# Two transfers instead of eight for each rotated projection, layer norms spread over two periods, and the MLP's gelu kept in its PSUM bank

## What is computed

```python
attn_in = adaln(x, cond, ln1, g1, b1)
x = attn(attn_in, attn_in, sa_wq, sa_wkv, sa_wo, sa_bo) + x
cross_in = adaln(x, cond, ln1, g1, b1)
x = attn(cross_in, ln(context), ca_wq, ca_wkv, ca_wo, ca_bo) + x
ffn_in = adaln(x, cond, ln2, g2, b2)
x = gelu(ffn_in @ ff_w1 + ff_b1) @ ff_w2 + ff_b2 + x

def attn(xq, ctx, ...):            # rope on q and k, softmax over 512 keys
    q, k, v = heads(xq @ wq), heads(ctx @ wk), heads(ctx @ wv)
    return softmax(rope(q) @ rope(k).T * DH ** -0.5) @ v @ wo + bo

def adaln(x, c, lw, lb, gw, gb, bw, bb):
    return ln(x, lw, lb) * (1 + c @ gw + gb) + (c @ bw + bb)
```

## Time and profile before

| | |
|---|---|
| median of 3 runs (range) | 1145.44 us (1144.98 to 1146.52) |
| the profiled execution | 1144.7 us, span of its instructions 1142.9 us |
| PE busy | 1099.4 us (96%) |
| DVE, POOL, ACT busy | 855.3, 774.0, 638.0 us (75, 68, 56%) |
| mean granted TensorE clock | 0.988 |

### The profile page before, as it was taken

How to read it: one execution, slowest core, us unless ns; L and a number is a source line. 1 busy time by engine, 2 the same in 40 slices (tenths; PEclk the granted TensorE clock), 3 DMA queues, 4 the chain that set the end, 5 groups by cost and what they waited for, 6 DMA issues and landing times.

```text
span 1142.9 us, 18646 instructions
## 1 busy us (share of the span) xinstructions
PE 1099.4 (96%) x6888; PEld 786.5 (69%) x6888; DVE 855.3 (75%) x1025; ACT 638.0 (56%) x895; POOL 774.0 (68%) x497
## 2 busy tenths in 40 slices
PE   7689999999999999999999999999999999989998
PEld 6456667776667777666766667776666667756887
DVE  5677787878787777778787777777787778676543
ACT  5455556665666555566565555555555555674521
POOL 3477788788678777688789766776777767654110
PEclk9799999999999999999999999999999999989999
DMA  6212111221221111211121112211121111300001
GB/s 183 61 30 75 38 41 45 70 48 34 51 73 40 38 38 31 59 38 38 26 64 38 38 38 50 58 33 32 31 70 38 38 38 38 93 1 1 20 19 37
DMA packets 65689, 52.36 MB, mean 46 GB/s; under 512 B 29120, under 2 KB 48576, under 8 KB 65344
## 3 DMA queue, kind: packets, MB, share of 16 engines
q1 hardware_dynamic: 63712, 49.59, 17.5%
q10 hardware_dynamic: 1888, 1.59, 0.5%
HBM read 15.22 MB, written 2.10 MB: 15 GB/s over the span
## 4 chain that ended last, share of the span: by engine, by line
PE 81%; DVE 7%; issue 4%; ACT 3%; POOL 2%; DMA 2%; SPq 2%; ACTq 0%; POOLq 0%; DVEq 0%
PE ps L862 16%; PE ps L711 11%; PE ps L712 10%; PE ps L713 10%; PE ps L809 6%; PE ps L840 5%; PE ps L850 5%; PE ps L815 5%; PE ps L811 5%; PE ps L813 4%; PE ps L945 3%; DVE neg_max L1036 2%; SPq L342 2%; DMA lo<-eo 1%; PE ps L727 1%
## 5 line engine op out<-in xcount | busy, mean ns | idle before, releaser
L537 ACT ACTIVATE probs<-ps 128x1024 f32<-128x1024 f32 x256 | 262.4, 1026 | 209.3 <-PE ps L815 185.5
L1036 DVE TENSOR_REDUCE neg_max<-ps 128x2 f32<-128x1024 f32 x256 | 301.7, 1225 | 80.9 <-PE ps L840 80.8
L412 POOL TENSOR_TENSOR acc<-acc,probs 128x1024 f32<-128x1024 f32 x128 | 304.6, 2380 | 17.7 <-POOL acc L407 0.4
L862 PE MATMUL ps<-probs,v 128*64 128x512 f32 x1024 | 230.7, 592 | 0.0
L407 POOL TENSOR_TENSOR acc<-probs 128x1024 f32<-128x1024 f32 x64 | 152.5, 2383 | 82.1 <-ACT probs L537 82.1
L417 POOL TENSOR_TENSOR eo<-tmp 128x512 f32<-128x512 f32 x62 | 89.2, 1439 | 137.9 <-DVE tmp L1063 129.0
L862 PEld LDWEIGHTS ps<-probs,v 128*64 128x64 f32 x1024 | 73.6, 137 | 145.8 <-issue 145.8
L1063 DVE TENSOR_TENSOR tmp<-ps,rope 128x1024 f32<-128x1024 f32 x128 | 150.6, 1212 | 3.5 <-PE ps L713 2.6
L809 PE MATMUL ps<-max_rows,pick 64*128 64x512 f32 x512 | 110.5, 422 | 11.1 <-DVE o_lo L1050 6.0
L840 PE MATMUL ps<-hi 64*128 64x512 f32 x512 | 106.8, 408 | 14.1 <-ACT hi L551 7.8
L711 PE MATMUL ps<-xn_hi,w_hi 128*128 128x512 f32 x256 | 108.2, 423 | 0.0
(11 more groups left out here) (113 smaller groups left out, 2269.1 us busy)
## 6 DMA issues: line engine op xcount, KB each, us to landing
lo<-eo SPq DMA_DIRECT2D x512, 64.0 KB, 2.0
w_raw<-pack_dram SPq DMA_DIRECT2D x16, 192.0 KB, 3.2
x<-x_dram SPq DMA_DIRECT2D x4, 512.0 KB, 10.8
w_raw<-pack_dram SPq DMA_DIRECT2D x8, 256.0 KB, 3.7
max_rows<-neg_max SPq DMA_DIRECT2D x128, 2.0 KB, 2.0
w_raw<-w_dram SPq DMA_DIRECT2D x2, 1024.0 KB, 5.6
out<-x SPq DMA_DIRECT2D x4, 512.0 KB, 2.9
ctx_in<-ctx_dram SPq DMA_DIRECT2D x4, 384.0 KB, 3.6
```

The costliest lines, as they stand in the source:

```text
L412: pool.tensor_tensor(acc[:, g % 2, :, :], acc[:, g % 2, :, :], probs[:, i, :, :], ALU.add).then_inc(added, 1)
L537: act.activation(probs[:, i, :, :], score_ps(i), ACT.Exp, scale=SCALE).then_inc(exped, 1)
L862: mm = pe.matmul(av_ps[DH * h:DH * h + DH, :], v[:, u % 2, kt, c:c + DH], probs[:, kt, h, :], start=(kt == 0), stop=(kt == TT - 1))
L1036: dve.tensor_reduce(neg_max[:, g % 2, :, i], peak_ps(i), AX.X, ALU.max, negate=True).then_inc(maxed, 1)
```

## The change

1. `land` issues two DMAs a job instead of eight: one for each pair, 64 partitions of `eo` with both halves, into all 128 partitions of `raw_qk`. It waits for both halves first. Rows of q and k come to lie in another order of partitions (the same in both).
2. Norms in periods: `guess_rstd` goes to behind `keep_av`, `norm_rows` to the next period, behind `guess_inverse` and ahead of `high_qk`. This holds for the context's norms too. `norm_stats` goes behind `normalise`, and `refine_rstd` behind the third `add_probs`.
3. The MLP's gelu is written back to its PSUM bank, `hid` is gone; `split_hid` reads PSUM; `hidden` waits for `hid_split`. The last two norms come one block earlier, with a gelu between their halves, and `refine_rstd(LAST)` moves from DVE to POOL.
4. The opening: 10 and 6 products of constants (`warm`) on PE; `modulate` in four parts, the second norm's two later; job 1 turned into a buffer of its own; another order on every engine; x of batch entry 3 and the context loaded later; `cols` waits apart from `ctx_ln`.

```diff
+        def eo_of(j):
+            return acc[:, 1, :, :] if j == 1 else eo
...
         def job_ps(j, e):
-            return ps[:, (2 if j == 3 else 3) + e, :]
+            return ps[:, 3 + e, :]
+        def hid_ps(f):
+            return ps[:, (f + 3) % 4, :]
         def ln_ps(n, r):
-            if n == 2:
-                return ps[:, r, :]
...
-        norm_at = {NB - 1: (0, 0, 1, True)}
+        norm_at = {NB - 1: (0, 1, 1)}
...
-            norm_at[norm_of(X, 1, b)] = (p, p, p + 1, True)
-        norm_at[norm_of(X, 2, 0)] = (PAIRS - 5, PAIRS - 5, PAIRS - 4, True)
-        norm_at[norm_of(X, 2, 1)] = (PAIRS - 3, PAIRS - 3, PAIRS - 2, True)
+            norm_at[norm_of(X, 1, b)] = (p, p + 1, p + 1)
+        norm_at[norm_of(X, 2, 0)] = (PAIRS - 5, PAIRS - 4, PAIRS - 4)
+        norm_at[norm_of(X, 2, 1)] = (PAIRS - 3, PAIRS - 2, PAIRS - 2)
...
             def land(j):
-                sp.wait_ge(rotated, 2 * j + 1)
+                sp.wait_ge(rotated, 2 * j + 2)
...
-                    for e in range(2):
-                        if a == 0 and e == 1:
-                            sp.wait_ge(rotated, 2 * j + 2)
-                        for h in range(2):
-                            rows = DH * h + 32 * e
-                            at = 32 * (2 * a + h)
-                            sp.dma_start(raw_qk[rows:rows + 32, g % 4, k, :], eo[at:at + 32, e, :])\
-                              .then_inc(landed, 16)
+                    sp.dma_start(raw_qk[:, g % 4, k, :], eo_of(j)[64 * a:64 * a + 64, :, :]).then_inc(landed, 16)
...
             load_weights(0)
-            for b in range(1, NB):
-                sp.dma_start(x[:, b, :, :], x_d[b].rearrange("(t p) d -> p t d", p=128)).then_inc(x_in[b], 16)
-            load_ctx(0)
+            load_x(1)
+            load_x(2)
             land(0)
             land(1)
             land(2)
             land_max(0)
+            load_x(3)
+            load_ctx(0)
             land(3)
...
@@ POOL, period(p) @@
                     add_probs(p, 2)
-                if n is not None and norm_at[n][3]:
-                    refine_rstd(pool, n)
                     add_probs(p, 3)
+                if p in stats_in:
+                    refine_rstd(pool, stats_in[p])
...
@@ ACT, period(p) @@
                     guess_inverse(p - 1)
+                if p in rows_in_period:
+                    norm_rows(rows_in_period[p])
                 if is_pair(p + 2):
                     high_qk(p + 2)
                 if p in split_in:
                     split_weights(*split_in[p])
-                if at_once:
-                    guess_rstd(n)
-                    norm_rows(n)
                 if is_pair(p - 1):
                     high_o(p - 1)
                 if is_pair(p):
                     keep_av(p)
+                if p in stats_in:
+                    guess_rstd(stats_in[p])
+                if p in turned_in:
+                    norm(turned_in[p], 0)
+                    norm(turned_in[p], 1)
...
             def gelu(b, f):
                 act.wait_ge(hid_mm, 8 * b + f + 1)
-                if f >= 4:
-                    act.wait_ge(hid_split, 8 * b + f - 3)
-                act.activation(hid[:, f % 4, :], ps[:, (f + 3) % 4, :], ACT.Gelu,
+                act.activation(hid_ps(f), hid_ps(f), ACT.Gelu,
...
@@ PE, opening @@
+            warm(10)
             modulate(0)
+            modulate(1)
             norm(0, 0)
             norm(0, 1)
             turn_rope()
-            modulate(1)
+            warm(6)
             project(0)
+            project(1)
             norm(1, 0)
             norm(1, 1)
-            project(1)
             project_v(0, 0)
             project_v(0, 1)
+            modulate(2)
             project(2)
+            peak(0, 0)
+            peak(0, 1)
+            peak(0, 2)
+            peak(0, 3)
+            modulate(3)
+            project(3)
             norm(2, 0)
             norm(2, 1)
-            for i in range(TT):
-                peak(0, i)
-            project(3)
...
@@ DVE, opening @@
-            modulate(1)
             rotate(0, 0)
-            norm_stats(2)
             rotate(0, 1)
             turn(0)
             rotate(1, 0)
             rotate(1, 1)
             turn(1)
+            norm_stats(2)
             rotate(2, 0)
             rotate(2, 1)
             for i in range(TT):
                 peak(0, i)
             low_qk(0)
+            modulate(1)
             rotate(3, 0)
...
@@ DVE, period(p) @@
-                if n is not None:
-                    norm_stats(n)
                 if is_pair(p - 1):
                     normalise(p - 1)
+                if p in stats_in:
+                    norm_stats(stats_in[p])
+                if is_pair(p - 1):
                     low_o(p - 1)
...
@@ PE, mlp(b) @@
                 def hidden(f):
                     if f >= 4:
-                        pe.wait_ge(hid_ready, 8 * b + f - 3)
+                        pe.wait_ge(hid_split, 8 * b + f - 3)
+                    elif b > 0:
+                        pe.wait_ge(hid_split, 8 * (b - 1) + f + 5)
```

More of the change, by code:

```diff
@@ L434, in period @@
                     add_probs(p, 2)
-                n = stats_in.get(p)
-                if n is not None and norm_at[n][3]:
-                    refine_rstd(pool, n)
-                if is_pair(p):
                     add_probs(p, 3)
-                if n is not None and not norm_at[n][3]:
-                    refine_rstd(pool, n)
+                if p in stats_in:
+                    refine_rstd(pool, stats_in[p])
                 if p in split_in:
@@ L457, in _ @@
             refine_rstd(pool, 2)
+            rotate(2)
             low_weights(pool, 0, 3)
-            rotate(2)
             norm_split(pool, 2, 0)
@@ L593, in period @@
                     split_weights(*split_in[p])
-                n = stats_in.get(p)
-                at_once = n is not None and norm_at[n][3]
-                if at_once:
-                    guess_rstd(n)
-                    norm_rows(n)
                 if is_pair(p - 1):
@@ L602, in period @@
                     keep_av(p)
-                if n is not None and not at_once:
-                    guess_rstd(n)
-                turned = turned_in.get(p)
-                turned_late = turned is not None and norm_at[turned][0] == p
-                if turned is not None and not turned_late:
-                    norm(turned, 0)
-                    norm(turned, 1)
+                if p in stats_in:
[3 more added lines that the diff above has]
+                    norm(turned_in[p], 1)
                 if p in v_in:
                     keep_v(v_in[p], 0)
-                if turned_late:
-                    norm(turned, 0)
-                if p in v_in:
                     keep_v(v_in[p], 1)
-                if turned_late:
-                    norm(turned, 1)
-                n = rows_in_period.get(p)
-                if n is not None and not norm_at[n][3]:
-                    norm_rows(n)
                 if p in (PAIRS - 3, PAIRS - 2):
@@ L670, in _ @@
             norm_rows(LAST - 1)
-            for f in range(3, 7):
-                gelu(0, f)
+            gelu(0, 3)
+            gelu(0, 4)
+            gelu(0, 5)
             norm(LAST - 1, 0)
+            gelu(0, 6)
             norm(LAST - 1, 1)
@@ L679, in _ @@
             norm_rows(LAST)
-            for f in range(1, 7):
+            for f in range(1, 6):
                 gelu(1, f)
             norm(LAST, 0)
+            gelu(1, 6)
             norm(LAST, 1)
@@ L879, in period @@
                     pe.wait_ge(maxed, 4 * (p + 1) + 4)
-                n = turned_in.get(p)
-                at_once = n is not None and norm_at[n][0] == p
-                if n is not None and not at_once:
-                    norm(n, 0)
-                    norm(n, 1)
+                if p in turned_in:
+                    norm(turned_in[p], 0)
+                    norm(turned_in[p], 1)
                 if is_job(p + 4):
@@ L896, in period, with warm @@
                     project_out(u - 1, 1)
+            def warm(count):
+                pe.wait_ge(const_ready, 6)
+                for _ in range(count):
+                    pe.matmul(ps[:, 1, :], pick[:, :], max_rows[:, :], start=True, stop=True)
+            warm(10)
             modulate(0)
+            modulate(1)
             norm(0, 0)
@@ L931, in hidden @@
                     for kt in range(KT):
-                        mm = parts(ps[:, (f + 3) % 4, :], w1_hi[:, kt, cut], w1_lo[:, kt, cut],
+                        mm = parts(hid_ps(f), w1_hi[:, kt, cut], w1_lo[:, kt, cut],
                                    xn_hi[:, b, kt, :], xn_lo[:, b, kt, :], kt == 0, kt == KT - 1)
@@ L1108, in period @@
                     rotate(p + 4, 1)
-                if n is not None and is_pair(p + 2):
+                if is_pair(p + 2) and p in stats_in:
                     low_qk(p + 2)
```

100 lines of the change are left out of this document (51 added, 49 removed).

## The result

The changed kernel takes 1118.61 us (median of 4 runs, 1118.14 to 1118.73) against 1145.45 us for the kernel before beside it: the ratio is 0.9764, 95% interval 0.9747 to 0.9781, so 27 us less. The forecast was 1119.7. The sum was right; its terms were not, and this is what the experiments are about.

What follows compares the result with a forecast made beforehand. PE's own work was taken to bound two thirds of the kernel, the prize lying in its idle time elsewhere. 13.0 + 5.0 + 2.5 + 4.5 = 25.0 off 1144.7 gave 1119.7 us, range 1111 to 1130 (own 1113 to 1124).

Steps and rivals of the forecast that it cites:

- Part 1: Two transfers a job instead of eight: 4.9 us in the opening against 6.9, 5.5 against 6.9 in the periods.
- The rival of a landing over 6.2 us: 256 KB transfers land late, PE waits in each of 32 quads and the kernel gets slower, 1177 at 8 us; chance 0.03.
- In the periods it hides behind PE: In the periods the shorter transfers save PE nothing; they only move SP's queue to the better.
- Part 2, the opening: Opening up to period 1: gains 4.6, 3.5, 4.8 and 1.3, less 1.2, sum 13.0 us.
- near 55: Sign in the opening: `score(1, 0)` would come near 55 us instead of 68.
- All 24: Jobs 0 and 1, 24 products at 0.43 us instead of 0.23: all would give 4.8 us; 3.5 taken with DVE's relief.
- Against this: `modulate(1)` and `rotate(3)` ... -1.2: Opening: both now stand between the maxima and `peak(1, 0)`, costing 1.2 us, an estimate at one rotation.
- The opening gives only half: Rival: clock stays half through jobs 0 to 1, another chain ends the opening; 13.0 becomes 6.5, 1126 us; chance 0.15.
- Part 3: Norms over two periods: 4.6 of 5.6 us idle back in 467 to 600, plus 0.4 in 68 to 467: 5.0.
- The rival of 11 new waits: Rows ahead of `high_qk` cost 0.6 us in each of 11 norms, period 62 stays as it is: 1129; chance 0.10.
- Part 4: Periods 59 to 62: PE's 4.71 us wait for `o_lo` gives 1.8, what follows 0.7: 2.5 us.
- Part 5: MLP with gelu in PSUM: 4.5 of the 5.2 us waits for `hid_lo` gained, some 0.5 left at the first `down`.

Runs made afterwards that it cites:

- period 61 turned round: Changed kernel with DVE's `low_o` ahead of `norm_stats` in period 61: 1120.67 us, ratio 0.9783, against 1118.68 for the version with `rotate(3)` ahead of `norm_split`.

## Why the forecast was right in sum and wrong in its terms

In short: the forecast of 1119.7 is near 1118.6 by luck, since its terms are off by up to 4.2 us and cancel. **The reading of the bound held.** PE was full in two thirds of the kernel, and 1 to 27 and 35 to 59 didn't move (+0.2 and -0.6). All the gain lies in the four stretches named.

**Part 1.** From the end of the turn's first half to the landing, 4.9 us was taken: 0.7 + 1.2 + 3.0. Measured: an issue 0.6, a landing 3.2 in the median and 3.6 for the second of a job, 3.8 for that of job 1, inside the bounds of 2.0 and 3.7 but for that; for job 1 the way is 6.1, since POOL held the second half of the turn. The rival of a landing over 6.2 us is out. What failed is "In the periods it hides behind PE": the two transfers alone gave 3.9 us in 27 to 35. PE's old waits there were put down to `issue` or to DVE, and I read them as the norms' alone; ACT's 10.0 us of waiting for landings stood behind them.

**Part 2, the opening: 13.0 forecast, 8.8 measured.** Marks of before against after: `hi` 40.82 and 33.86; first scores 51.15 and 46.71; pair 0's average 56.66 and 53.10; `score(1, 0)` 68.08 and 60.49 (the sign "near 55" was missed); pair 1's average 75.32 and 66.55. So, step by step:

- up to `hi`: 7.0 of the forecast 4.6 + 3.5 = 8.1. The turn of job 1 starts at 26.97, where the working gives 30.6 - 3.5 = 27.1, but it takes 2.5 instead of 1.4, and its landing 3.8 instead of 3.0. The split in two terms was wrong: the own buffer is worth 0.5 to 0.8 by its run, not the 3.07 of the old wait, since with two transfers the landing that it waited for comes sooner, and DVE is held by POOL where it would have waited. "All 24" products at half clock was wrong too: in the kernel before, job 1's twelve already ran at full clock, 0.24 us from one to the next (rows below), so 2.4 us at most were to be had and not 4.8, and by the run without constant products they were worth nothing at `hi`.
- the wait for `av`: 4.0 of 4.8 (0.75 is left). It is the norms' order that takes it: with that alone PE's idle time between the two averages goes from 4.8 to 1.5.
- the half clock behind it: 1.2 (from `score(1, 0)` to the average 7.24 and 6.06), as taken, 1.3.
- **the step that failed is "Against this: `modulate(1)` and `rotate(3)` ... -1.2"**: it was 3.4. From `hi` to the first scores it takes 12.85 us instead of 10.33. I had priced what DVE does there and not what PE does. PE's `modulate(3)` stands between the maxima and `project(3)` and takes 1.7 at half clock (`modulate(2)`, as many products, took 0.95 at full clock), and norm 2's transposes, which before ran at 33.06 inside PE's wait for `hi` of 7.8 us, now stand behind `project(3)` and take 1.0. From the first scores to the average it is 6.39 instead of 5.51, since ACT scales norm 2 ahead of the exponentials. Some 0.9 of the 3.4 is this execution's: in the version with period 61 turned round, whose opening is the same code, the clock rises in the middle of `project(3)` and the way from `hi` to the first scores is 11.9.

PE before: job 1 at full clock, norm 2's transposes, `project(3)`, the first scores (start, length, instruction):

```profile
24.55 0.39 PE L712 MATMUL ps<-xn_lo,w_hi 128*128 128x512 f32 x1
24.79 0.40 PE L713 MATMUL ps<-xn_hi,w_lo 128*128 128x512 f32 x1
...
33.06 1.09 PE L727 MATMUL ps<-ident,z 128*128 128x128 f32 x8
...
45.94 0.79 PE L711 MATMUL ps<-xn_hi,w_hi 128*128 128x512 f32 x1
...
51.15 0.50 PE L809 MATMUL ps<-max_rows,pick 64*128 64x512 f32 x2
```

PE of the changed kernel, from `modulate(3)` to the first scores, with `project(3)` between:

```profile
38.91 1.86 PE L686 MATMUL ps<-cond,probs 128*128 128x4 f32 x8
40.63 0.77 PE L701 MATMUL ps<-xn_hi,w_hi 128*128 128x512 f32 x1
...
45.74 1.04 PE L717 MATMUL ps<-ident,z 128*128 128x128 f32 x8
46.71 0.50 PE L800 MATMUL ps<-max_rows,pick 64*128 64x512 f32 x2
```

This account is read from the two traces; the run that moved `project(3)` did not turn it into a gain, because DVE's and ACT's chain ended in the same place. So 46.7 for the first scores is held from two sides, and which of them would give way to a better order stays open.

The rival *The opening gives only half* (6.5) is nearer to 8.8 than the forecast's 13.0. Its condition, half clock through jobs 0 and 1, did not come; its other half, another chain that ends the opening, did.

The rule of the Trainium skill (TensorE: Matmul & The Clock Gate, section Part 4: PE-mode transpose) had `warm(10)` lost before `project(0)`. The trace agrees in what it shows: `modulate(0)` and `modulate(1)` (3.58 us) and the eight transposes behind them (1.95, at full clock 1.03) take the same with `warm(10)` ahead of them as without, all at half clock, and full clock begins inside `warm(6)`, whose first two products start 0.44 us apart and the next ones 0.23. `warm(6)` alone was not run, and the two together didn't change the time.

**Part 3, 5.0 forecast, 7.4 measured.** I took 4.6 of 5.6 us idle. All but 0.3 of the idle time was given back, and some 2 us more, at a clock of 1.00 in both: PE's busy time fell too, from 127.36 for 804 products to 125.70 for 807 (between the same two averages, 27 and 35, from 126.9 to 124.7). Part of the surplus is the transfers': with the norms' order alone 27 to 35 was 5.8 shorter, with all of it 7.6. A product of the maxima behind a wait is recorded as busy for longer (0.62, usually 0.40), so a wait costs more than its idle time. The 0.4 in the first 27 periods did not come (+0.2). The rival of 11 new waits did not come either.

**Part 4, 2.5 forecast, 3.1 measured.** The wait was to shrink by 1.8 and shrank by 2.0, from 4.71 to 2.73; what follows gave 1.1 and not 0.7, since PE's clock in 59 to 63 is 0.97 instead of 0.94. "DVE's statistics and `normalise` now do" was the right cause, but the statistics stand there for a reason: behind `low_o` they hold ACT.

**Part 5, 4.5 forecast, 6.7 measured.** Right in each step (no long ones, 0.69 a cast, one wait of 0.4), too small in size: I counted the waits, 5.2 less some 0.5 (4.7, put down as 4.5), and not the half clock after them. The waits gave 4.8. PE's busy time for the same 638 products fell by 1.9, from 102.49 to 100.58; before, the clock had fallen behind the first of the three waits (0.83 granted from 1040.6 to 1050.6 us) and not behind the other two. This second part is not certain in every execution, as the two transfers' run above shows.

So the sum came out by compensation: 4.2 too much in the opening, 2.4 + 0.6 + 2.2 too little elsewhere, and 0.6 of scatter: 25.0 - 4.2 + 5.8 = 26.6, the difference of the two spans. One small slip in the working: the upper ends of the gains, 6 + 6.5 + 5 + 5.5 with the opening's other 9.5, make 32.5 and so 1112, not 1111.

## What to carry to other kernels

Price a step that is moved on every engine that it occupies, PE too, and ask which wait covered it where it was. A wait of PE costs more than its idle time: add the longer first product and, where the clock falls, the half clock behind it, which the granted clock of the stretch shows. Since the clock doesn't fall behind such a wait in every execution, compare idle time and busy time of a stretch apart before its length is put down to a change. Before an engine is made faster, look at what holds the next one: here PE's 1.3 us ended in front of a DVE that POOL held. Before an operation that holds up a queue is moved back, look at who waits for its result in order on another engine.

## What the runs showed of the hardware

- DVE is held by POOL even for 128 x 4 elements. In period 29 of the changed kernel the `var_eps` operation, 0.17 us in 12 of its 16 cases, took 1.08 and ended at 501.97, as POOL's addition in SBUF ended at 501.95. DVE and POOL:

```profile
500.89 1.08 DVE L1031 TENSOR_SCALAR var_eps<-mean_var 128x4 f32<-128x4 f32 x1
```

```profile
497.02 4.93 POOL L414 TENSOR_TENSOR acc<-acc,probs 128x1024 f32<-128x1024 f32 x2
```

- The same code behind the same waits doesn't always lose the clock. In period 62, after waits of 1.56 and 2.70 us, the four `total` products took 1.84 in one kernel and 1.08 in the other, and from pair 61's average to pair 62's it was 15.9 and 14.3 us. With period 61 turned round alone, and with `rotate(3)` moved too:

```profile
997.88 1.84 PE L843 MATMUL ps<-acc,ones 128*64 128x512 f32 x4
```

```profile
998.28 1.08 PE L843 MATMUL ps<-acc,ones 128*64 128x512 f32 x4
```

- 256 KB between two tiles of SBUF land 3.2 us after the issue in the median (3.6 for the second of a job), 64 KB 2.0; so two transfers of 256 KB beat eight of 64 KB by the issues saved, not by the landing.
